# Two layers of convolutional attention on one core: the second layer's step on TensorE takes both first-pass pairs and both score halves together, then all biases, the single jobs and the values

## What is computed

```python
qkv = jnp.einsum('oc,bcn->bon', w_qkv, xf)
q, k, v = jnp.split(qkv, 3, axis=1)
...
sim = jnp.einsum('bhdi,bhdj->bhij', q, k) * scale
bias = _cpb_bias(H, cpb_w0, cpb_b0, cpb_w1, cpb_b1, cpb_w2, cpb_b2)
sim = sim + bias[None]
attn = _stable_softmax(sim)
out = jnp.einsum('bhij,bhdj->bhdi', attn, v)
...
return out + residual
```

## Time and profile before

| | us |
|---|---|
| median of 3 runs | 4899.85 |
| lowest, highest | 4897.66, 4905.59 |
| the profiled execution | 4941.7 |
| its span, first to last instruction | 4939.7 |
| PE busy | 4250.2 (86%) |
| DVE busy | 2960.9 (60%) |
| ACT busy | 2420.8 (49%) |
| POOL busy | 517.8 (10%) |

### The profile page before, as it was taken

How to read it: one execution, slowest core, us unless ns; L and a number is a source line. 1 busy time by engine, 2 the same in 40 slices (tenths; PEclk the granted TensorE clock), 3 DMA queues, 4 the chain that set the end, 5 groups by cost and what they waited for, 6 DMA issues and landing times.

```text
span 4939.7 us, 69414 instructions
## 1 busy us (share of the span) xinstructions
PE 4250.2 (86%) x27098; PEld 1111.1 (22%) x27098; DVE 2960.9 (60%) x8660; ACT 2420.8 (49%) x2830; POOL 517.8 (10%) x819
## 2 busy tenths in 40 slices
PE   7755378888888888799989999999999999999998
PEld 2111011221212122222222222222222222222222
DVE  5433255555555555577766776667767667776771
ACT  3322134444444445425555556655555555555555
POOL 2101212111121211111000000000000000000000
PEclk6555555555555556669999999999999999999999
DMA  1499910000000020012222222222232222232321
GB/s 41 29 57 56 61 14 12 9 12 7 12 12 9 12 58 12 5 32 70 67 66 67 57 79 68 74 56 68 69 83 59 75 58 73 63 80 56 85 56 36
DMA packets 262672, 236.15 MB, mean 48 GB/s; under 512 B 215129, under 2 KB 218057, under 8 KB 262089
## 3 DMA queue, kind: packets, MB, share of 16 engines
q1 hardware_dynamic: 241544, 205.85, 22.7%
q0 software_dynamic: 20800, 25.87, 2.5%
HBM read 226.65 MB, written 27.19 MB: 51 GB/s over the span
## 4 chain that ended last, share of the span: by engine, by line
PE 75%; DMA 9%; DVE 8%; issue 5%; ACT 1%; POOL 1%; SPq 0%; POOLq 0%; ACTq 0%; DVEq 0%
PE P L588 23%; PE P L573 14%; PE P L535 12%; PE P L540 6%; PE P L554 6%; PE P L614 4%; DVE maxes L879 4%; DMA d_den<-sums 4%; PE P L558 4%; PE P L653 3%; DMA d_rden<-rden 2%; DVE junk L875 2%; DMA rwide<-d_rden 2%; DVE q_stack L912 1%; DMA den<-d_den 1%
## 5 line engine op out<-in xcount | busy, mean ns | idle before, releaser
L757 ACT ACTIVATE probs<-P 128x896 f32<-128x896 f32 (+1 forms) x2352 | 2124.7, 916 | 2017.2 <-PE P L573 1136.6
L875 DVE CUSTOM_DVE_ANT_0 junk<-P,mstage 112x448 bf16<-112x448 f32 x3136 | 1780.3, 621 | 757.0 <-PE P L535 756.5
L588 PE MATMUL P<-probs,vals 128*17 128x448 f32 (+1 forms) x9408 | 1381.7, 666 | 27.0 <-ACT sums L837 26.8
L879 DVE TENSOR_REDUCE maxes<-P 112x1 f32<-112x392 f32 x1792 | 898.5, 559 | 753.1 <-PE P L540 752.5
L540 PE MATMUL P<-keys,q_stack 24*112 24x392 f16 x1792 | 567.7, 513 | 400.6 <-DVE maxes L879 261.4
L573 PE MATMUL P<-bstage,flip 112*56 112x448 f16 x6272 | 905.0, 369 | 0.0
L535 PE MATMUL P<-keys,q_stack 48*112 48x448 f16 x3136 | 755.9, 408 | 121.8 <-DVE q_stack L912 51.2
L554 PE MATMUL P<-q_two,keys 49*128 49x448 f16 x3136 | 649.0, 358 | 0.0
L535 PEld LDWEIGHTS P<-keys,q_stack 48*112 48x112 f16 x3136 | 281.0, 126 | 1030.8 <-DVE maxes L875 493.3
L423 POOL DMA_DIRECT2D d_den<-sums x84 | 49.5, 589 | 3081.2 <-ACT sums L837 3081.2
L573 PEld LDWEIGHTS P<-bstage,flip 112*56 112x56 f16 x6272 | 212.2, 105 | 589.1 <-issue 589.1
(11 more groups left out here) (124 smaller groups left out, 1520.2 us busy)
## 6 DMA issues: line engine op xcount, KB each, us to landing
mstage<-g_max SPq DMA_DIRECT2D x56, 1519.0 KB, 7.9
bstage<-g_bias SPq DMA_DIRECT2D x28, 1568.0 KB, 8.2
bstage<-g_bias SPq DMA_DIRECT2D x28, 1519.0 KB, 7.8
rwide<-d_rden POOLq DMA_DIRECT2D x336, 56.0 KB, 2.1
g_max<-t_bf SPq DMA_DIRECT2D x16, 673.8 KB
g_bias<-t_hi SPq DMA_DIRECT2D x8, 679.9 KB
g_bias<-t_lo SPq DMA_DIRECT2D x8, 679.9 KB
wg<-in_wg POOLq DMA_DIRECT2D x12, 386.0 KB, 3.3
```

The source lines that it names most:

```text
L588: last = mm(P[32 * h:32 * h + HD + 1, PV, 0:QB], table[0:kr, kt, h, :], probs[0:kr, s % 3, h, :], start=kt == 0, stop=kt == unit.tiles - 1 ...
L757: A(probs[0:kr, s % 3, 2 * p:2 * p + 2, :], P[0:kr, 2 * p:2 * p + 2, 0:QB], ACT.Exp).then_inc(exp_done, 1)
L875: V.tensor_tensor_reduce(out=junk[:, PLAN.nth[job] % 4, :], in0=P[0:QT, bank_of(job), 0:QB], in1=bias, scale=1.0, scalar=-3.0e38, op0=ALU. ...
L879: V.tensor_reduce(out=maxes0[:, unit.i % 2, t, 2 * p + r, c:c + 1], in_=P[0:QT, bank_of(job), 0:HALF], op=ALU.max, axis=AX.X).then_inc(max ...
```

## The change

The loop of TensorE is rewritten for steps of layer 1: for each half first pass and scores, then `biases` of half 0 and half 1, then the jobs of the step, then the values. Jobs which the plan put at half "a" of such a step are now put at half "b", for all engines; that concerns "s" (the turning of the maxima). The order of the ring is that of the plan, so first-pass matmuls keep their places in it; an "s" job, which stood between pair a and pair b, now stands after pair b. Steps of layer 0 stay as they are.

```diff
--- before.py
+++ after.py
@@ -95,7 +95,10 @@
                 self.pairs[places[k * len(places) // len(unit.work)]].append((unit, k, *what))
 
     def place_jobs(self):
-        put = lambda s, w, *job: self.jobs[s, w].append(job)
+        def put(s, w, *job):
+            inside = 0 <= s < LAST and STEPS[s][0].biased
+            self.jobs[s, "b" if inside else w].append(job)
+
         for n in range(2):
             put(-12, "ab"[n], "k", 0, n, 0)
         put(-11, "a", "v", 0, 0)
@@ -727,12 +730,14 @@
                             first_pass(*pair)
                     if inside:
                         scores(s, p)
-                    if biased:
-                        biases(s, p)
-                    else:
+                    if not biased:
                         for pair in PLAN.pairs[s, w]:
                             first_pass(*pair)
-                    beside(s, w)
+                        beside(s, w)
+                if biased:
+                    biases(s, 0)
+                    biases(s, 1)
+                    beside(s, "b")
                 if 1 <= s <= LAST:
                     values(s - 1)
 
```

## The result

| | us |
|---|---|
| before, median of 4 runs | 4902.47 |
| after, median of 4 runs | 5338.69 |
| ratio | 1.0854, 95% interval 1.0820 to 1.0889 |
| the profiled execution after, and its span | 5332.8, 5330.9 |

The change makes the kernel 8.5% slower, 436 us. The forecast was 348 us more, that is 5248; the range reached to 5380.

The account below looks back on a forecast made before the run. Bound: b1's wait for VectorE's maximum of a0, with biases 0 moved out of that wait. Terms 318 + 19 - 15 + 6 + 20 = +348 us on 4899.85 gave 5248 us; range 5195 to 5380.

Parts of the forecast that it names:

- The chain a0, maximum, b1: Second-layer step: the fourth first-pass matmul (b1) waits for VectorE's maximum of the first (a0), 1.12 us from start to start.
- The plain step: Ordinary second-layer step on TensorE: from 3.01 to 3.43 us, times 756 steps, +318 us.
- the price of a bias pair: TensorE, plain step: each of the two bias pairs moved behind b1 adds 0.21 us.
- Changes of kind: TensorE switching between kinds of matmul: about 0.07 us each; two saved a step, worth nothing because they lay ahead of b1.
- The rival that forecast a gain: If b1 did not wait as read, steps shrink: 784 x 0.14 = 110 us, about 4790 us; chance 2%.
- The sums: Step 1 of a unit: values wait for ScalarE's copy of the sums, +0.69 us x 27 = +19 us.
- The reciprocal: VectorE waits for a DMA at step 3 of a unit, pair b of step 4 for VectorE: -15 us, at best -22.
- The last unit: Unit without first pass: the two exponentials set steps of 2.68 instead of 2.46 us, +0.22 x 28 = +6 us.
- The granted clock: TensorE's clock in the second layer: lower-level share from 5.6% to 7.5%, +20 us, bounds 0 and +103.
- after each fall in the second layer the clock came back soon: Argument against the slow-clock rival: quick recovery in the second layer, hence its mean clock of 0.97.
- The clock's rival: Waits hold the clock down for long: a fifth of the stage low gives 5386 us, all about 6750; chance 9%.
- the forecast's own case: The summed terms, 5248 us, bounds 5221 and 5331 (15% at the lower clock level); chance 85%.

Follow-up runs that it names:

- e5: The kernel after with pair b moved behind all eight biases: 4695.7 us, 0.9572 of the kernel before.
- e6: The kernel of e5 with pair b between the biases of half 0 and of half 1: 4829.2 us, 0.9804 of the kernel before.
- the first profiled execution: The kernel before, unchanged, profiled for the forecast: 4941.7 us.
- the one before again: The kernel before, unchanged, profiled a second time: 4894.2 us.

## Why the prediction was right, and where a term was off

*The chain a0, maximum, b1.* Right, and shown four ways: 1.12 us from a0 to b1 in the trace after; 1.12 with work put into the wait; the step shrinks by as much as the maximum does; and with the biases back inside, the loss is gone.

*The plain step.* The mechanism was right, the size a little too large: 3.38 us and not 3.43. The term failed in the price of a bias pair, which I took as 0.21 (0.49 less 0.28). The eight biases after take 0.87 from their start to the values (3815.75 to 3816.62). With 0.28 for the change, 0.59 are left for three spacings: 0.21 for the first and 0.19 for each later one in the trace, and the two moved pairs are such later ones. 756 x 0.38 = 287 us instead of 318.

*Changes of kind.* Right that their saving is lost here: in the step after they lie in the wait. They are worth more than the 0.07 us that I read, where they are on the path: 0.12 a change by e5 against e6. The rival that forecast a gain had a true price in the wrong place. Its sum, 784 x 0.14, also leaves out the 0.10 of b1's wait that its own sentence names: with it a step gains 0.24, and the order of e5, which does free b1, gained 0.22.

*The sums.* PE's idle time ahead of step 1's values is 1.16 us against 0.42; +0.74 for a forecast of +0.69, some 20 us.

*The reciprocal.* The long waits for maxima are gone as forecast: the longest is now 1.0 us, where it was 2.0 and the one of step 4 took 1.40. What that gave was not measured apart; the forecast had 15, at best 22.

*The last unit.* From its first scores (5229.10 after, 4796.61 before) it takes 6 us longer, as forecast, and its exponentials start 2.68 us apart, as forecast (5239.99 and 5242.67).

*The granted clock* was the term that failed in size: +20 us forecast, with bounds of 0 and 103. From the means, the lower level had 2 x 0.02 = 4% of 2625 us before (105 us) and 2 x 0.07 = 14% of 3036 after (425 us). Priced as in the forecast, 425 x (1 - 3.38/5.47) less 105 x (1 - 3.01/5.16) is 162 - 44 = 118 us. The means are rounded, and by the 143 us at the lower level in the first profiled execution it would be 103: so some 100 to 120. Filling the wait gave back 78 us of the stage. The step of the argument that failed was "after each fall in the second layer the clock came back soon": I took the recovery of the kernel before as given and let the share grow from 5.6% to 7.5% only. In the new order the clock fell 59 times where it had fallen 18 to 27 times, and stayed low for 7 us on average where it had been about 5. The new wait is there at the lower level too: in the row at 3804.82 the two matmuls start 0.55 us apart (1.17 less 0.62). The profile counts no idle time there, and which part of the wait holds the clock down was not tested apart. The clock's rival, which I gave 9%, is thus about half true: a share of 14% where the forecast had 7.5% and the rival 20%. Its last figure is a slip: all of the stage at the lower level comes to 4899.85 + 328 + 1535 - 62 = 6701 us, not 6750.

*Sum.* 287 for plain steps, 118 for the clock, 20 for the sums and 6 for the last unit, less up to 22 for the reciprocal, make 409 to 431 us; the stage and the last unit grew by 417. Against the first profiled execution they grew by 396, and with 103 for the clock the terms make 394 to 416. The first layer was 21 us longer in the execution after than in the one before again; that is within what two executions of the kernel before differ by there (26), so I don't count it. What is left of the 436 between medians is of that size too, and stays open.

So the mechanism was right. The forecast was 91 us short, and two errors in it partly cancel, which is luck: plain steps were 31 us too dear, the clock some 80 to 100 us too cheap; the remaining 20 to 40 us are the open rest. The measured 5339 lies 8 us above the bound of the forecast's own case, 5331, and inside the range only because that was drawn on into the clock's case.

## What to carry to other kernels

Where an instruction waits for a buffer that another engine frees, ask what stands between the instruction that filled the buffer and the one that wants it: work put there was free here up to that latency (1.12 us), and work moved from there to behind the wait cost its full time, even on an engine that showed no idle time. Grouping matmuls of one kind is worth having (0.12 of the 0.22 us a step that the order with pair b last gains; the old order without its wait takes 2.90, this one 2.78), but only where the ring's distance in time is kept; and here a wait in every step had a second price, the granted clock: 100 to 120 of the 436 us.

## What the runs showed of the hardware that I had not expected

- TensorE's price for a change of kind depends on the kinds, start to start: 0.19 us from pair to pair within one kind (0.21 for the first after a change), 0.28 from scores (49 rows, 128 columns) to biases (112 rows, 56 columns) and from biases to first pass, 0.33 from first pass (48 rows, 112 columns) to biases or to values. The Trainium skill, TensorEngine Tiling (Array Packing), Key Properties, says that a change of tiling mode drains TensorE. These rows agree with it: such a change took 0.09 to 0.14 us more than 0.19. No run here separates the drain from other causes, such as the loading of another shape of weights.
- Added matmuls made the kernel faster: four more in each step, in a wait, and the median was 106 us lower; in the profiled executions 78 us of it lie in the stage, whose granted clock went from 0.93 to 0.97.
- Profiled executions of one kernel differed by 47 us (4941.7 and 4894.2), a good half of it in the first layer, where the clock is at 0.57.
